# Ternary weights turned during the attention, a one-product low-rank term, and the output projection inside the feed-forward block

## The reference, cut to what matters

```
x = x + attention(layernorm(x)) @ Wo                         # 16 heads of 16; 4 sequences of 1024
x = x + ffn(layernorm(x))
def bitlinear(x, w):  scale = clip(mean(|w|, axis=1), 1e-5)   # one scale for each row of w
                      return x @ (clip(round(w / scale), -1, 1) * scale).T
h = bitlinear(x, w_fc) + gate * (x @ v.T @ fast_b.T @ u.T)   # 256 -> 1024; the second term has rank 16
ffn = bitlinear(relu(h) ** 2, w_proj)                         # 1024 -> 256
x = x + state_space_layer(...);  x = x + mixture_of_experts(...)   # not touched
```

## Time and profile before

| | |
|---|---|
| time, median of 3 | 1728.4 us |
| profiled execution: time, span | 1726.34 us, 1724.6 us |
| granted TensorE clock, mean | 0.919 |
| PE busy | 1524.6 us (88%) |
| DVE busy | 1177.8 us (68%) |
| ACT busy | 979.8 us (57%) |
| POOL busy | 433.5 us (25%) |

### The profile page before, as it was taken

The page is one execution under the profiler, slowest core; times in us unless marked ns, Lnnn a source line. Parts: engine busy times, 40 slices in busy tenths (PEclk is TensorE's granted clock), DMA queues, the critical chain, the costliest instruction groups (busy, mean ns, idle before and its releaser), DMA issues. The chain is left out here.

```text
span 1724.6 us, 40236 instructions
## 1 busy us (share of the span) xinstructions
PE 1524.6 (88%) x14143; PEld 1004.6 (58%) x14144; DVE 1177.8 (68%) x2254; ACT 979.8 (57%) x2029; POOL 433.5 (25%) x682
## 2 busy tenths in 40 slices
PE   6999999999999999998699966999785499999990
PEld 5843333333333333336588865888673199999980
DVE  7688999999999999912578857554467822222225
ACT  3427888888888888880345512444222055555543
POOL 3055201101010101000112237222221045555540
PEclk9968999999999999997899976999896599999995
DMA  6950232333232323010100002333109432222218
GB/s 213 304 142 16 45 62 48 69 54 61 48 69 45 59 45 58 9 22 20 13 1 1 1 14 51 102 101 101 51 16 326 152 114 70 71 69 73 70 58 292
DMA packets 122967, 135.26 MB, mean 78 GB/s; under 512 B 29300, under 2 KB 93832, under 8 KB 122696
## 3 DMA queue, kind: packets, MB, share of 16 engines
q1 hardware_dynamic: 110056, 107.60, 24.3%
q0 software_dynamic: 7584, 20.72, 3.7%
q10 hardware_dynamic: 5184, 4.98, 0.8%
HBM read 92.23 MB, written 36.04 MB: 74 GB/s over the span
## 5 line engine op out<-in xcount | busy, mean ns | idle before, releaser
L1912 DVE TENSOR_REDUCE mx<-ps 128x1 f32<-128x1024 f32 x512 | 622.7, 1221 | 24.6 <-PE ps L2059 18.8
L1950 ACT ACTIVATE PR<-ps 128x512 f32<-128x512 f32 x1024 | 557.1, 599 | 87.4 <-PE ps L2113 37.5
L2059 PE MATMUL ps<-KQ 48*128 48x512 f32 x1024 | 389.1, 462 | 4.0 <-DVE mx L1912 3.6
L2113 PE MATMUL ps<-KQ 50*128 50x512 f32 x1024 | 379.9, 450 | 0.0
L2095 PE MATMUL ps<-PR,VO 128*32 128x256 f32 x4096 | 330.2, 394 | 9.1 <-ACT PR L1950 8.7
L2113 PEld LDWEIGHTS ps<-KQ 50*128 50x128 f32 x1024 | 155.2, 187 | 216.9 <-ACT PR L1950 199.6
L2095 PEld LDWEIGHTS ps<-PR,VO 128*32 128x32 f32 x4096 | 81.0, 108 | 196.0 <-ACT PR L1950 99.5
L2059 PEld LDWEIGHTS ps<-KQ 48*128 48x128 f32 x1024 | 158.9, 192 | 21.3 <-DVE mx L1912 20.6
L1804 PEld LDWEIGHTS ps<-e_xinT,e_w 128*128 128x128 f32 x1264 | 155.0, 194 | 5.8 <-issue 1.9
L1804 PE MATMUL ps<-e_xinT,e_w 128*128 128x128 f32 x1264 | 155.8, 277 | 1.1 <-ACT e_xinT L1736 1.1
L1794 PE MATMUL ps<-eW,e_hiddenT 128*128 x632 | 149.4, 380 | 0.0
(11 more groups left out here) (274 smaller groups left out, 2098.5 us busy)
## 6 DMA issues: line engine op xcount, KB each, us to landing
qk_parts<-parts SPq DMA_DIRECT2D x8, 2048.0 KB, 8.4
TB<-toeplitz_lines SPq DMA_DIRECT2D x32, 512.0 KB, 6.5
KQ<-qk_parts SPq DMA_DIRECT2D x96, 128.0 KB, 4.6
KQ<-qk_parts SPq DMA_DIRECT2D x192, 64.0 KB, 2.4
eW<-in_L_ffn_W SPq DMA_DIRECT2D x16, 512.0 KB, 6.9
eW<-in_L_ffn_W SPq DMA_DIRECT2D x8, 1024.0 KB, 13.2
e_got<-expert_outputs SPq DMA_DIRECT2D x16, 512.0 KB, 9.6
X<-in_L_attn_x SPq DMA_DIRECT2D x8, 512.0 KB, 4.4
```

Source lines behind the costliest of these rows:

```text
L1912: nc.vector.tensor_reduce(mx[:, u % RING, h * QT + q:h * QT + q + 1], ps[:, b:b + 2].rearrange("p a n -> p (a n)"), AX, ALU.max, negate=Tr ...
L1950: nc.scalar.activation(PR[:, kt % 2, h], ps[:, st_bank(u, s)], ACT.Exp).then_inc(exp_done, 1)
L2059: made = nc.tensor.matmul(ps[:, max_bank(u, t) + k], of_tile(queries(u % RING), h, q), kq[half(h, KROWS), 0, h % HR, k * BANK:(k + 1) * BA ...
L2113: nc.tensor.matmul(ps[:, st_bank(u, s)], kq[half(h, AROWS), 0, h % HR, kt * P:(kt + 1) * P], queries(u % RING)[half(h, AROWS), qc, h % HR] ...
```

## The change

- `quantise` writes w > scale/2 minus w < -scale/2 as bf16 for both matrices, into a buffer of their own (`ternary`). The row scale of w_fc now goes into the relu (`activation(..., Relu, scale=sc)`).
- GpSimd gets `low_rank_rows` in unit 2: u times gate over the row scale, as parts side by side (80 columns).
- In the last attention unit the slots of `again` are taken by 44 steps of `turn` (8 transposes of the low-rank rows, 4 small fp32 products, 32 transposes of bf16 weights), then by one `again` product a slot. VectorE's `keep` takes the results out of PSUM, after its last row maxima.
- The projection stage is gone. The feed-forward block begins with it: `heads_out` 0 to 5, the transposes and `low_rank` of chunk 0, `heads_out` 6 and 7, with `add_heads` on VectorE between its first statistics.
- In a body, block m has 4 products of 512 columns (ternary w_fc is exact in one part) and one `correct` product of 80 rows, issued after the 4 of m + 1. `low_rank` (4 products of 512 columns to 80 rows) for the next chunk stands in `outputs`, after its third quarter; ScalarE and VectorE split its result (`low_rank_high`, `low_rank_low`).
- The output of two chunks ago is copied out of PSUM by ScalarE at m = 2 (`copy`), and GpSimd multiplies it by the row scales (4 instructions) before its 4 additions. VectorE's `scale` is gone.

The diff, cut to its core:

```diff
 def quantise
-            times = (sc[:, 1, r:r + 1], ALU.mult) if r < FK else (None,)
-            step(nc.gpsimd.tensor_scalar(up, w, sc[:, 2, r:r + 1], times[0], ALU.is_gt, *times[1:]))
+            step(nc.gpsimd.tensor_scalar(up, w, sc[:, 2, r:r + 1], None, ALU.is_gt))
...
-            step(nc.gpsimd.tensor_tensor(w, up, w, op=ALU.subtract))
+            step(nc.gpsimd.tensor_tensor(self.ternary[r][:, cols], up, w, op=ALU.subtract))
+    def low_rank_rows(self, nc, pool, ident):
+        step(nc.gpsimd.tensor_tensor(sc[:, 2, 0:FK], sc[:, 1, 0:FK], sc[:, 3, 0:FK], op=ALU.pow))
+        for k in range(FK):
+            steps.mark(nc.gpsimd.tensor_scalar(u[:, k], u[:, k], self.gate[:], sc[:, 2, k:k + 1], ALU.mult, ALU.mult))
...
+    def turn(self, nc, pe, ps, n, ident, identb):
+        if n < 8:
+            last = nc.tensor.transpose(ps[0:LOW, n // 4, ...], self.u5[:, n].bitcast(F32), ident[:])
...
+        elif n < 28:
+            last = nc.tensor.transpose(half_bank((3, 0)[half])[...], self.tp[:, o, kk * P:(kk + 1) * P], identb[:])
+        else:
+            last = nc.tensor.transpose(half_bank((1, 3)[half])[...], self.tf[:, k, half * P:(half + 1) * P], identb[:])
+    def keep(self, nc, dve, ps, steps):
...
+            nc.vector.tensor_copy(self.wfT[0][:, half], half_bank(bank)).then_inc(self.kept, 1)
-def output_projection(...)
...
 feed_forward, gpsimd
-                for c in range(2):
-                    norm.root(pool, c, c)
+                norm.root(pool, 0, 0)
+                weigh_heads(pool, UNITS // 2 - 1)
+                norm.root(pool, 1, 1)
                 def add(c):
-                    pool.wait_ge(o_scaled, c + 2)
+                    pool.wait_ge(o_copied, c + 2)
                     for k in range(CT):
+                        nc.gpsimd.tensor_tensor(scaled[:, k], scaled[:, k], pscale[:], op=ALU.mult).then_inc(o_weighted, 1)
+                    for k in range(CT):
+                        pool.wait_ge(o_weighted, CT * c + k + 1)
                         nc.gpsimd.tensor_tensor(tile, scaled[:, k], tile, op=ALU.add).then_inc(o_added, 1)
 feed_forward, vector
+                def low_rank_low(c):
+                    dve.wait_ge(t_hi, c + 1)
+                    nc.vector.tensor_tensor(tT[LATE:LOW], ps[LATE:LOW, T_BANK], tT[LATE:LOW].bitcast(F32), op=ALU.subtract).then_inc(t_ready, 1)
-                        if m == 3 and not (isinstance(c, int) and c < 2):
-                            scale(c - 2)
                     if more(c, 1):
                         low(c + 1, 1 - h)
                     sq_low(c, h, FK - 1)
+                    if more(c, 1):
+                        low_rank_low(c + 1)
 feed_forward, scalar
-                        nc.scalar.activation(relu[:, m % 2], ps[:, 2 + m % HB], ACT.Relu).then_inc(relu_ready, 1)
+                        nc.scalar.activation(relu[:, m % 2], ps[:, 2 + m % HB], ACT.Relu, scale=sc[:, 1, m:m + 1]).then_inc(relu_ready, 1)
+                        if m == 2 and not (isinstance(c, int) and c < 2):
+                            copy(c - 2)
 feed_forward, tensor
+                def low_rank(c, h):
+                    pe.wait_ge(xl_ready, c + 1)
+                    for a in range(2):
+                        for dk in range(DK):
+                            last = nc.tensor.matmul(ps[0:LOW, T_BANK], fvT[:, a, dk], xT[a][:, h, dk], ...)
+                    last.then_inc(t_done, 1)
+                for c in range(6):
+                    heads_out(c)
                 turn(0, 0)
+                low_rank(0, 0)
+                for c in range(6, NC):
+                    heads_out(c)
                 def body(c, h):
-                    pe.wait_ge(xl_ready, c + 1)
                     for m in range(FK):
                         pe.wait_ge(relu_ready, FK * c + m + 1)
-                        todo = [p for dk in range(DK) for p in split_products([w[:, dk, m * P:(m + 1) * P] for w in wfT], [x[:, h, dk] for x in xT])]
+                        todo = [(wfT[:, dk, m * P:(m + 1) * P], x[:, h, dk]) for dk in range(DK) for x in xT]
...
+                        if m > 0:
+                            correct(c, m - 1)
+                    correct(c, FK - 1)
                     if not is_first(c):
-                        outputs(c - 1, 1 - h)
+                        outputs(c - 1, 1 - h, c)
+                    else:
+                        low_rank(c + 1, 1 - h)
+                def correct(c, m):
+                    if m == 0:
+                        pe.wait_ge(t_ready, c + 1)
+                    nc.tensor.matmul(ps[:, 2 + m % HB], uT[:, m * P:(m + 1) * P], tT[:], start=False, stop=True).then_inc(h_done, 1)
+                def outputs(c, h, now):
                     for k in range(CT):
...
+                        if k == 2 and more(now, 1):
+                            low_rank(now + 1, h)
 attention, tensor
-                    again(ahead, k)
+                    beside_the_last(QC * (ahead - MAXES * UNITS) + k, ahead, k)
```

More of the change, by code:

```diff
@@ L484, in __init__ @@
         self.nmT = sbuf(stack, "nmT", [P, QC, P // 4])
+        self.words = RING * HG * QT + QC * 2 * PARTS * HR * QH + QC * P // 4
 class FeedForwardWeights:
     def __init__(self, sbuf, stack):
-        self.wfT = [sbuf(stack, f"wfT{a}", [P, DK, FH], F32R) for a in range(2)]
+        self.wfT = [sbuf(stack, "wfT0", [P, DK, FH], F32R)]
+        with ExitStack() as split:
+            self.wfT.append(sbuf(split, "wfT1", [P, DK, FH], F32R))
+        ternary = sbuf(stack, "ternary", [P, FK * D + DK * FH], BF16)
@@ L540, in quantise @@
                 step(nc.gpsimd.tensor_scalar(sc[:, k], sc[:, 1], f, None, ALU.mult))
-        blocks = [(r, w[:, n:n + D]) for r, w in enumerate(self.rows) for n in range(0, w.shape[-1], D)]
-        for r, w in blocks[quarter * len(blocks) // 4:(quarter + 1) * len(blocks) // 4]:
-            up = above[:, 0:D]
-            times = (sc[:, 1, r:r + 1], ALU.mult) if r < FK else (None,)
-            step(nc.gpsimd.tensor_scalar(up, w, sc[:, 2, r:r + 1], times[0], ALU.is_gt, *times[1:]))
-            step(nc.gpsimd.tensor_scalar(w, w, sc[:, 3, r:r + 1], times[0], ALU.is_lt, *times[1:]))
-            step(nc.gpsimd.tensor_tensor(w, up, w, op=ALU.subtract))
@@ L550, in output_projection @@
-def output_projection(nc, sem, sbuf, ps, X, slot, weighed, invert_sums, spread_inverses, weigh_heads, ident, ffw):
-    wfT, wpT, pscale, wf, wp, u, fb, v, gate, sc = ffw.wfT, ffw.wpT, ffw.pscale, ffw.wf, ffw.wp, ffw.u, ffw.fb, ffw.v, ffw.gate, ffw.sc
-    with ExitStack() as s0:
-        o_done, o_added = sem("a_done"), sem("a_added")
-        uT = sbuf(s0, "uT", [RANK, FH])
-        fbT = sbuf(s0, "fbT", [RANK, RANK])
-        fv = sbuf(s0, "fv", [RANK, D])
-        spread = sbuf(s0, "spread", [P, DK, P])
-        f_rows, f_tr, f_lr, f_kept, t_done, t_hi, t_lo, s_spread = (
-            sem(n) for n in ("ffn_rows", "lowrank_tr", "lowrank_done", "lowrank_kept", "ffn_w_tr", "ffn_w_hi", "ffn_w_lo", "ffn_spread"))
+        blocks = [(r, slice(n, n + D)) for r, w in enumerate(self.rows) for n in range(0, w.shape[-1], D)]
@@ L766, in body @@
                     sq_high(c, h, FK - 1)
-                chunks(act, body)
+                    if more(c, 1):
+                        low_rank_high(c + 1)
+                chunks(act, body, first=True)
+                copy(NC - 2)
+                copy(NC - 1)
             @block.tensor
@@ L1996, in gpsimd @@
                     ffw.quantise(nc, pool, kept, QC * u + qc)
+                if u == 2 and qc == 0:
+                    ffw.low_rank_rows(nc, pool, ident)
             if 0 < u < UNITS - 1:
```

331 lines of the change are left out of this document (188 added, 143 removed).

## The result

The changed kernel took 1771.77 us (median of 4 runs: 1776.71, 1773.10, 1750.69, 1770.44), the kernel before 1726.79 us beside it. The ratio is 1.0243, 95% interval 1.0155 to 1.0331: slower by some 45 us, where 11.8 was forecast and the range ended at 1754. The profiled execution took 1776.71 us, with a span of 1775.0 (before 1724.6), so the two profiles differ by 50.4 us.

The account below looks back on a forecast made before the run. The prediction took DVE to close the feed-forward loop as tightly as PE. The start's -23.4 and the loop's +35.2 gave +11.8 us on the profiled 1726.3, which lies 2.1 under the median, so 1740; range 1720 to 1754.

Parts of the forecast that it names:

- the last unit: Last attention unit: 44 `turn` steps replacing `again` products change its time by 0, bounds -4 and +4 us.
- the last unit goes cold: Rival, last attention unit: transposes keep the clock down, a pair costs 2.16 us instead of 1.23; +20, 1760; chance 0.11.
- The start: Start of the feed-forward up to body 0: removing the projection stage brings body 0 to 820.0 from 843.4, -23.4 us.
- 1.9 us there for a clock that the rest in front of `low_rank` would drop: Start of the feed-forward: 2.7 us of rest before `low_rank` probably drops the clock, costing 1.9 us.
- The loop: Feed-forward bodies: each steady chunk takes 26.7 us against 19.95 as DVE waits on a longer chain; +35.2 us.
- Its three terms: Steady chunk: DVE's first square to `low` 18.1 us, `low` to next first square 6.2, cold restart 2.4.
- S2: First square of body 2, put at 865.2 us, with PE resting only 2 us before it.
- DVE's circle: Feed-forward loop: DVE's work plus the way from `low` to the next first square sets the period, 19.9 us before.
- Contention: Feed-forward loop: eight GpSimd instructions instead of four slow DVE's two-input instructions, +2.1 us a chunk.
- The clock holds: Rival, loop: no cold restarts, or contention grows little; 1728, 1735 or both 1723; chance 0.22 with milder contention.
- The +9.8 us outside the changed stretches: Up to the end of the attention and the stages behind the feed-forward: forecast unchanged, 0.

Follow-up runs that it names:

- again_beside: The changed kernel with a 50-row `again` product issued beside `turn` steps 4 to 43 except 8 and 9; 1749.0 us, ratio 1.0153 to the kernel before.
- turns_alone: The changed kernel with `again` beside steps 4 to 7, 10 and 11 only; 1759.73 and 1746.59 us, ratio 1.0152 to the kernel before.
- weights_in_unit: late_turns with the 32 bf16 weight transposes put into the last unit, the other twelve steps staying at the feed-forward's start; 1716.62 us, ratio 0.9938.
- first_in_unit: late_turns with the first twelve steps put into the last unit, then `again`, the 32 transposes staying at the feed-forward's start; 1718.13 us, ratio 0.9942.
- fill: The changed kernel with 24 idle products in front of `low_rank` in each body (some outputs wrong); 1758.50, 1767.35, 1766.94 and 1735.13 us.
- early_low: The changed kernel with the next chunk's split (normalisation, transposes, `high`, `low`) moved forward in each body; 1746.82 us, median of 9 runs.
- late_only: late_turns without the next chunk's split moved forward, so the loop is as in the changed kernel; 1751.21 us, ratio 1.0125.
- late_turns: early_low with all 44 `turn` steps moved between the feed-forward's first chunks of heads, last unit as before the change; 1713.08 us, ratio 0.9912.

## Why the prediction was wrong, and where it was right

- **The step that failed** is the last unit: "In the last unit 44 `turn` steps replace `again` products ... I take 0, bounds -4 and +4." It measured +35.7. Two errors are in it. First, the price: I reasoned from the 0.10 us of a 128-column product in a run of its like the earlier trace rows and from PE's busy time, in which `again` counts in full. Yet `again` cost nothing, since it ran beside the scores on other rows (tail 37.2 us with it and without it), so replacing it saved nothing and each step came on top with 0.27 to 0.33 us: 12.6 us, three times my bound (again_beside). Second, the term took the unit's clock to stay at 1.00. It was 0.50 for 58 us, 23.1 us of the loss.
- **The rival "the last unit goes cold"** (0.11, 1760) named the right event, with a cause that is right only in part and too small a price. It priced cold pairs with `again` (2.16); those with transposes take 2.89. What stood against it, that the score and PV products stay and are most of PE's time, failed: PE was busy 20.00 of 20.00 us at 0.50. The bulk of the transposes doesn't lower the clock: 32 of them hold 1.00 (turns_alone, weights_in_unit). The first steps lower it when no `again` stands beside them (first_in_unit, against turns_alone). By the Trainium skill, "TensorE: Matmul & The Clock Gate", Part 4: PE-mode transpose, a transpose doesn't count as busy in the same way as a product. The traces agree in part: the 32 transposes beside scores and PV products did not lower a full clock, but they did not raise a lowered one either in 45 us (758 to 803 in the changed kernel), while it came back 7 us after the last step there, and 10 us after it in first_in_unit, with `again` in the slots.
- **The start** held: -25.7 for -23.4, since body 0 came 34.4 us behind the first product of the heads, for 36.6 predicted. The sum had 1.9 us there for a clock that the rest in front of `low_rank` would drop; the rest was 2.36 us and the clock stayed at 1.00.
- **The loop** held in mechanism and nearly in size: +30.5 for +35.2. Its three terms measured 17.6 for 18.1, 6.2 for 6.2 (fill), and 2.4, 1.3, 2.3 and 1.1 (8.58, 7.53, 8.54 and 7.30 less 6.2) for 2.4 four times. The four steady periods sum to 102.4 us for 106.8: 4.4 of the missing 4.7. Smaller misses cancel: S2 came 46.6 us behind the start of body 0 for 45.2, since body 1's rest of 2.15 us dropped the clock too, where the sum had no cold restart, and body 6 and the end took 1.3 less. That DVE's circle and not PE bounds it is shown by early_low: PE's work is the same and the period falls to 20.0 us.
- **Contention** held in kind and was sized too high: in a chunk three squares and three low parts took 1.11 and 1.23 us beside GpSimd (959.70 to 966.6), where it was one square and two low parts before (954.78 to 958.3). The rows of before give 0.54 + 0.42 + 0.53 = 1.5 us for these, where the sum read about 2.0; at some 0.48 us each the three more are 1.4 us, for +2.1 in the sum; the 0.7 between them covers the 0.5 us by which 17.6 lies under 18.1.
- **"The clock holds"** was wrong in the loop: rests of 4.55 to 4.59 us, shorter than the 5.15 of the earlier trace rows, dropped it each time, and so did 3.74 us in body 6 and 2.15 in body 1. But length alone doesn't decide: 1.77 us held it in fill and 1.82 us dropped it in late_only, and 2.36 us at the start of the stage held it in the changed kernel and dropped it in late_turns (`low_rank` 1.15 and 1.99 us).
- The +9.8 us outside the changed stretches, forecast as 0, are within what the profiles of all kernels vary by there (14.7 and 11.7 us). For the 3.4 up to the last reduction the clock between 130 and 180 us shows it; for the 6.4 behind it is argued only.

Open: which property of the first steps lowers the clock, and why `again` beside them prevents it. Either part of the twelve alone left it up in one profiled run, which doesn't exclude a chance. Whether one kernel has a cold unit in some runs and not in others isn't shown: the run of 1750.69 us of the changed kernel (mean clock 0.917 against 0.898 to 0.904) lies 20 to 26 us under its others, about what the cold unit costs, but no trace of it was kept.

## What to carry to other kernels

A filler product that runs on other rows beside real work was free here; before you replace it by useful work, ask whether the new instruction fits beside the same neighbours. If it needs the whole array, price it at the slot it opens and not at its own pace among its like, and put it where it can run packed (6.7 us here, for 12.6 spread out at full clock and 35.7 with the clock lost). A clock that held before can be lost although TensorE never rests, so read the granted clock of the stretch after such a change. In a loop closed by two engines, the producer that the next round waits for belongs as early in its engine's order as its inputs allow: moving the next chunk's split forward, with not one instruction taken away, was worth 32 us.

## What the runs showed of the hardware that was not expected

- TensorE busy in every microsecond of a window (20.00 of 20.00, 760 to 780) still had clock 0.50, which lasted 58 us in all (752 to 810).
- A 128-column bf16 transpose between a 50-row product and eight 32-column PV products costs 0.27 us at full clock and (2.89 - 2.16) / 2 = 0.37 at half, against 0.06 in a row of its like (late_turns: 16 between 796.75 and 797.64).
- The same first steps of `turn` (ten in three profiles, eleven in fill) lowered the clock with no `again` beside them and did not with a few beside them (four profiles of four each).
- Rests of TensorE of nearly one length ended at either clock: 2.36 us at 1.00 and at 0.50, 1.77 us at 1.00, 1.82 us at 0.50.
- Early in the attention the clock between 130 and 180 us was 0.59 to 0.94 over the profiles, and the last reduction came up to 14.7 us later with it. The times of one kernel, early_low, went from 1710.58 to 1752.38 us.
- At half clock `low_rank` took 2.00 us for 1.09.
